# Attention scores from separate products of queries and keys, in place of one product with a matrix fused at setup

## The chip, the core and the metric

The kernel runs on one core of a Trainium2 chip. The metric is device time in microseconds (us) of one launch, inputs and outputs in HBM; lower is better. TensorE is called PE in the rows, its weight loads PEld, VectorE DVE, ScalarE ACT, GpSimd POOL, SyncE (which issues the DMAs) SP.

## The reference, cut to what matters

```python
# x: (2, 2048, 640), ctx: (2, 128, 384); 8 heads of 80; fp32
enc, ca = ctx[:, :124], ctx[:, 124:]                 # 124 text tokens, 4 image tokens
hs = mha(x @ Wq, enc @ Wk, enc @ Wv)                 # text attention
ca_q1 = einsum('btc,th->bch', ca, Wq_ca)[:, indices] # indices: 384 rows spread over 2048
ca_hs1 = mha(ca_q1, x, x)                            # image attention, keys and values are x
ca_hs2 = mha(ca_hs1 @ Wq, ca @ Wk_ca, ca @ Wv_ca)    # 4 keys
out = (hs + ca_hs2) @ Wout + b_out + x
```

`mha` splits the columns by head, scales by 80 ** -0.5, and takes a softmax over the keys.

## The kernel before, in words

One batch entry (an "image", b = 0, 1) is 16 tiles of 128 rows of x. Each image passes through three stages, and setup stands ahead of the first.

**Precision.** Large products run in fp32r. A factor is split into a high part, rounded to fp32r, and a low part, the rest; three products (high x high, low x high, high x low) make one. So each matrix exists as a pair `_hi`, `_lo`: ScalarE writes the high part out of PSUM, VectorE the low one. Setup's products are plain fp32, where one product is two instructions on TensorE.

**Setup** (L1001 to L1057 on TensorE, L559 to L576 on ScalarE, L719 to L763 on VectorE). Scores x @ Wq @ K^T of a head are x @ (Wq_h K_h^T), so setup transposes the context (L1010), makes keys for each head (`kT_part`), transposes Wq (L1039), and multiplies it with the keys of both images: 40 products of 256 columns (L1057). The evictions write `mm_hi` and `mm_lo`, the fused matrix: for each of KT = 5 chunks of 128 rows of x's width it has 2 heads and the columns for g in one part (280 columns), and three heads, with some columns for y, in each of two others (372, 396 or 420 columns). `g_columns` and `y_columns` on GpSimd fill the columns for g (what the image attention needs of Wq_ca) and y (what the last attention needs of its four keys). The part for image 1 is kept in HBM (`raw_kept`) and split in image 0's output stage (`next_high`, `next_low`). The value products of both images (L1147, L1154) are the last of setup.

**Score stage** (`step`, L1103, once per tile). Three parts k = 0, 1, 2, each 5 chunks x 3 products into one PSUM bank; four banks are used in turn. Between those products stand, by a table written by hand (`AT`, L1101): the five transposes of the next tile of x (`xT`, L1070), the two transposes of the stacked g (`g_stack`, L1079), and six "units" (`unit`, L1096), each two products of 256 columns, whose largest value per row VectorE takes (L810). They bound the image attention's scores. After each part VectorE takes the least score per head (`least`, L777), ScalarE copies y (L593) and takes the exponentials with their sums (`exps`, L603), VectorE makes y's low part (L797), and GpSimd multiplies with the reciprocal sums (`normalise`, L492). The result is kept in HBM (`ex_kept`).

**Attention stage** (`sT`, L1194, and `pv`, L1216 and L1225), 32 quads: scores of four heads with 384 rows, exponentials on ScalarE into `e` (L648) and for each second quad into `e_hi` (L654), on VectorE `e_hi` for the others (L893) and always `e_lo` (L901), then products with `ybuf`. First come the transposes of `as_` (L1168), which need all units, and the rows of `aTs` made from them.

**Output stage**: transposed probabilities (`pT`, L1258), products with the value strips `vs_hi`, `vs_lo` (`heads_T`, L1309), with Wout (`output`, L1323), and the sum with x and bias (`add_x`, L958).

Each engine runs its list in the order of the code and waits on semaphores; nothing reorders it. The value strips are made by GpSimd (`value_strips`, L479) inside image b's score stage, after tile 0.

## Time and profile before

| | us |
|---|---|
| median of 3 runs | 797.14 (796.69 to 797.75) |
| the profiled execution, its own time | 797.15 |
| its span, first to last instruction | 795.4 |
| TensorE busy in the span | 772.5 (97%) |
| VectorE busy | 512.6 (64%) |
| ScalarE busy | 371.4 (47%) |
| GpSimd busy | 170.5 (21%) |
| mean granted TensorE clock, share of full speed | 0.991 |

Busy time of TensorE is the sum of modelled durations that overlap, since products are pipelined. What a product costs in a dense stretch is the distance from its start to the next start. In the tables by stage, "PEclk" is the mean of the clock that was granted, as a share of 2.4 GHz (its two levels are 1.2 and 2.4 GHz). The arrow at the end of a row says for how long the engine had been idle, and what ended that.

### The profile page before, as it was taken

How to read it: one execution, taken by the hardware profiler on the slowest of the kernel's cores; microseconds unless marked ns; L12 is line 12 of the kernel's file. 1: busy time of each engine (PE TensorE's matmuls, PEld its weight loads, DVE VectorE, ACT ScalarE, POOL GpSimd, SP SyncE). 2: the span in 40 equal slices, each digit the busy share in tenths (PEclk: the TensorE clock that was granted, in tenths of full speed). 3: DMA queues.
4: the chain of work that ended last, by engine and by line, in shares of the span. 5: the costliest groups of instructions: out<-in, count | busy, mean ns of one | idle time of the engine just before them, and what ended most of it. 6: DMA issues, size and time to landing. Idle time of an engine off the chain costs nothing.

```text
span 795.4 us, 13204 instructions
## 1 busy us (share of the span) xinstructions
PE 772.5 (97%) x5129; PEld 724.1 (91%) x5129; DVE 512.6 (64%) x878; ACT 371.4 (47%) x938; POOL 170.5 (21%) x232
## 2 busy tenths in 40 slices
PE   7999999999899999999999999999989999999998
PEld 5979999999777879999999999999968788999997
DVE  2446777676899986344545777676789996544432
ACT  1634444444489862233233444444469884222220
POOL 7025821222100001332220411222110001212130
PEclk9999999999899999999999999999989999999999
DMA  9123222222220024744422222222230003344431
GB/s 335 70 98 125 87 87 87 87 88 87 86 81 1 1 66 132 240 147 146 165 87 84 87 87 87 88 87 87 100 110 1 1 1 97 119 158 166 148 115 69
DMA packets 33462, 79.34 MB, mean 100 GB/s; under 512 B 8300, under 2 KB 9836, under 8 KB 33400
## 3 DMA queue, kind: packets, MB, share of 16 engines
q1 hardware_dynamic: 33400, 78.49, 29.0%
q8 instruction: 41, 0.67, 0.3%
q14 instruction: 21, 0.17, 0.1%
HBM read 48.56 MB, written 29.88 MB: 99 GB/s over the span
## 4 chain that ended last, share of the span: by engine, by line
PE 92%; DVE 4%; issue 2%; ACT 1%; DMA 0%; SPq 0%; DVEq 0%
PE PS L1124 30%; PE PS L1323 17%; PE PS L1309 8%; PE PS L1096 6%; PE PS L1194 5%; PE PS L1225 5%; PE PS L1216 5%; PE PS L1258 4%; PE PS L1057 2%; PE PS L1070 2%; PE PS L1017 2%; PE PS L1291 1%; DVE e_hi L893 1%; PE PS L1242 1%; PE PS L1079 1%
## 5 line engine op out<-in xcount | busy, mean ns | idle before, releaser
L1124 PE MATMUL PS<-mm_hi,xT_hi 128*128 128x280 f32 (+3 forms) x480 | 161.8, 337 | 0.0
L810 DVE TENSOR_REDUCE mpart<-PS 128x4 f32<-128x512 f32 x192 | 132.0, 688 | 42.0 <-PE PS L1096 41.8
L1124 PE MATMUL PS<-mm_lo,xT_hi 128*128 128x280 f32 (+3 forms) x480 | 157.8, 329 | 0.0
L1124 PE MATMUL PS<-mm_hi,xT_lo 128*128 128x280 f32 (+3 forms) x480 | 157.0, 327 | 0.0
L492 POOL TENSOR_TENSOR ex<-ex,rinv 128x992 f32<-128x992 f32 x32 | 59.1, 1847 | 240.2 <-DVE rinv L804 240.1
L1124 PEld LDWEIGHTS PS<-mm_hi,xT_hi 128*128 128x128 f32 x480 | 90.5, 189 | 0.6 <-issue 0.5
L1124 PEld LDWEIGHTS PS<-mm_hi,xT_lo 128*128 128x128 f32 x480 | 90.6, 189 | 0.3
L1124 PEld LDWEIGHTS PS<-mm_lo,xT_hi 128*128 128x128 f32 x480 | 90.3, 188 | 0.1
L603 ACT ACTIVATE ex<-PS,neg 128x124 f32<-128x124 f32 x256 | 89.9, 365 | 0.1
L901 DVE TENSOR_TENSOR e_lo<-e,e_hi 128x1536 fp32r<-128x1536 f32 (+1 forms) x46 | 77.3, 1689 | 4.9 <-ACT e_hi L654 4.1
L777 DVE TENSOR_REDUCE neg<-PS 128x3 f32<-128x372 f32 (+1 forms) x96 | 47.8, 498 | 48.3 <-PE PS L1124 48.3
L1096 PE MATMUL PS<-gT,aTm 128*128 128x256 f32 x384 | 76.6, 281 | 0.1
L1323 PE MATMUL PS<-wo_hi,oT_hi 128*128 128x320 f32 x320 | 75.4, 317 | 0.0
L1323 PE MATMUL PS<-wo_lo,oT_hi 128*128 128x320 f32 x320 | 72.9, 309 | 0.0
L1323 PE MATMUL PS<-wo_hi,oT_lo 128*128 128x320 f32 x320 | 72.8, 309 | 0.0
L648 ACT ACTIVATE e<-PS 128x1536 f32<-128x1536 f32 x44 | 64.2, 1459 | 14.8 <-PE PS L1194 14.8
L539 POOL TENSOR_TENSOR ex<-p2x,one 128x32 f32<-128x32 f32 x28 | 6.7, 241 | 300.5 <-ACT p2x L677 178.2
L688 ACT ACTIVATE oT_hi<-PS 128x256 fp32r<-128x256 f32 x80 | 30.8, 385 | 84.7 <-PE PS L1309 81.1
L958 DVE TENSOR_TENSOR res<-PS,xin 128x640 f32<-128x640 f32 x32 | 26.3, 823 | 67.9 <-PE PS L1323 67.8
L1194 PE MATMUL PS<-aTs,gT 128*128 128x384 f32 (+2 forms) x384 | 66.8, 314 | 1.9 <-DVE ybuf L797 1.5
L1096 PEld LDWEIGHTS PS<-gT,aTm 128*128 128x128 f32 x384 | 67.6, 188 | 1.2 <-DVE mpart L810 0.5
L593 ACT ACTIVATE ybuf<-PS 128x96 fp32r<-128x96 f32 x64 | 16.2, 254 | 108.9 <-DVE neg L777 108.9
(149 smaller groups left out, 1448.5 us busy)
## 6 DMA issues: line engine op xcount, KB each, us to landing
xin<-in_x SPq DMA_DIRECT2D x64, 320.0 KB, 3.5
ex_kept<-ex SPq DMA_DIRECT2D x32, 512.0 KB, 2.9
ex<-ex_kept SPq DMA_DIRECT2D x32, 512.0 KB, 3.9
out<-res SPq DMA_DIRECT2D x32, 320.0 KB, 2.3
raw_kept<-raw SPq DMA_DIRECT2D x5, 512.0 KB, 2.6
mm_lo<-raw_kept SPq DMA_DIRECT2D x10, 186.0 KB, 3.9
wq_in<-in_L_xattn_Wq SPq DMA_DIRECT2D x2, 800.0 KB, 8.9
wo_in<-in_L_xattn_Wout SPq DMA_DIRECT2D x1, 1600.0 KB, 8.0
```

The source lines that it names most:

```text
L492: nc.gpsimd.tensor_tensor(ex[:, i % 2, :, 0:NK], ex[:, i % 2, :, 0:NK], rinv[:, i % 2, :].unsqueeze(2).broadcast_to([P, NH, NK]), ALU.mult ...
L603: last = nc.scalar.activation(ex[:, i % 2, h, 0:NK], s_ps(T, h), ACT.Exp, bias=neg[:, i % 2, h:h + 1], scale=-1.0, accum_out=sums[:, i % 2 ...
L648: nc.scalar.activation(e_of(p), flat(sT_bank(p), 3), ACT.Exp, scale=SCALE).then_inc(e_made, 1)
L777: nc.vector.tensor_reduce(neg[:, i % 2, h0:h1], PS[:, slot(T, k), at:at + (h1 - h0) * NK].rearrange("p (h k) -> p h k", h=h1 - h0), AX.X, ...
L810: nc.vector.tensor_reduce(mpart[:, n // 2, :, 2 * (n % 2):2 * (n % 2) + 2, i].rearrange("p s k -> p k s"), PS[:, 6 + N % 2, :].rearrange(" ...
L901: nc.vector.tensor_tensor(e_lo[:, p % LO_BUFS, c0:c1], e_of(p)[:, c0:c1], e_hi[:, p % HI_BUFS, c0:c1].bitcast(F32), ALU.subtract)\
L1096: last = mul(PS[:, 6 + N % 2, k * G2:(k + 1) * G2].rearrange("p (s n) -> p s n", s=SETS), aTm[:, r0 + k, c * P:(c + 1) * P], gT[:, :, i * ...
L1124: last = mul(PS[:, slot(T, k), p0:p0 + w], l[:, i % 2, j, :], rr[:, m0:m0 + w], start=(j == 0 and n == 0), stop=(n == 2), skip_group_check ...
L1194: last = mul(flat(sT_bank(p), 3)[:, at:to], gT[:, s, kt * P:(kt + 1) * P], aTs[:, s, r, at - r * CAD:to - r * CAD], start=True, stop=True, ...
L1216: mul(PS[0:y_cols(r), 6 + r // 2, 0:CAD], y_of(kt, s * R + r), e_hi[:, p % HI_BUFS, r * CAD:(r + 1) * CAD], start=(kt == 0 and r % 2 == 0) ...
L1309: last = mul(PS[:, 6 + j % 2, 0:G2], strip(vv, j, h), pp[:, h, :], start=(n == 0 and k == 0), stop=(n == 2 and k + 1 == len(pieces[j])))
L1323: last = mul(PS[:, out_bank(2 * g + u) + f, 0:HALF], l[:, j, u * P:(u + 1) * P], rr[:, j, f * HALF:(f + 1) * HALF], start=(j == 0 and n == ...
```

## The change

Scores are made in two steps, for two tiles at a time (a "group" G, 8 per image). TensorE's order for a group is now:

- `y_part`: y and g of both tiles by themselves, from `yg_hi`, `yg_lo`, which hold for each chunk only the 2 or 3 heads that have rows in it ("pieces", 12 in all), 28 columns each.
- `q_part`: the queries of both tiles, transposed: Wq's chunks are the weights and the two tiles of transposed x the 256 columns. Evicted and split in two as `qT_hi`, `qT_lo`.
- `s_part`: four parts (tile u, heads 0 to 3 or 4 to 7): the transposed queries of a chunk are the weights, and the keys of that chunk's pieces the columns. In a piece the rows of other heads are zero (`headscale` holds the scale in a head's rows and zero in the others).

A unit is one product of 512 columns over both tiles; there are 12 per group, so 96 per image as before in columns, and half the instructions. The fused matrix, its round trip through HBM and the 40 products of setup are gone. Wq itself is split at setup and, since its low part's place is used again by the attention stage, once more for image 1. The value product of image b stands between its score stage and its attention stage, and with it GpSimd's value strips. Tile 1 of image 1 is transposed inside image 0's last output product.

TensorE, cut to the core:

```diff
-                        for j in range(KT):
-                            m0, w = mm_at(j, k)
-                            p0 = ps_at(j, k)
-                            for n, (l, rr) in enumerate(((xT_hi, mm_hi), (xT_lo, mm_hi), (xT_hi, mm_lo))):
-                                last = mul(PS[:, slot(T, k), p0:p0 + w], l[:, i % 2, j, :], rr[:, m0:m0 + w],
-                                           start=(j == 0 and n == 0), stop=(n == 2), skip_group_check=True)
...
+                def y_part(G):
+                    N = b * GROUPS + G
+                    pe.wait_ge(xTl_made, 2 * N + 2)
...
+                    for u in range(2):
+                        for j in range(KT):
+                            at, w = (u * NH + heads[j][0]) * YG, len(heads[j]) * YG
+                            for n, (l, rr) in enumerate(((xT_hi, yg_hi), (xT_lo, yg_hi), (xT_hi, yg_lo))):
+                                last = mul(PS[:, y_bank(N), at:at + w], l[:, u, j, :],
...
+                STACK_AT = 16
+                Q_AT = (32, 38, 44, 50, 56, 62, 68, 74)
+                S_AT = (6, 14, 22, 30)
...
+                def q_part(G):
...
+                    for c in range(KT):
+                        if N * KT + c >= 2:
+                            pe.wait_ge(ql_made, N * KT + c - 1)
+                        for j in range(KT):
+                            for n, (l, rr) in enumerate(((wq_hi, xT_hi), (wq_lo, xT_hi), (wq_hi, xT_lo))):
+                                last = mul(PS[:, q_bank(c), 0:G2].rearrange("p (u n) -> p u n", u=2), l[:, j, c * P:(c + 1) * P], rr[:, :, j, :],
+                                           start=(j == 0 and n == 0), stop=(j == KT - 1 and n == 2))
+                                if at == STACK_AT:
+                                    g_stack(G)
+                                if at in units_at:
+                                    unit(G, units_at.index(at))
...
+                def s_part(G):
...
+                        for c in range(KT):
+                            hs = [h for h in heads[c] if h // R == k]
+                            if not hs:
+                                continue
+                            pe.wait_ge(ql_made, N * KT + c + 1)
+                            m0 = piece_at[c] + heads[c].index(hs[0])
+                            to = hs[0] % R * NK
+                            for l, rr in ((qT_hi, kp_hi), (qT_lo, kp_hi), (qT_hi, kp_lo)):
+                                last = mul(PS[:, s_bank(2 * N + u, k), to:to + len(hs) * NK], l[:, c, u * P:(u + 1) * P],
+                                           rr[:, m0:m0 + len(hs), :].rearrange("p n k -> p (n k)"), start=first, stop=(hs[-1] % R == R - 1 and rr is kp_lo),
...
+                        if G + 1 < GROUPS and p % 2 == 0:
+                            xT(2 * G + 2 + p // 2)
...
+                pe.wait_ge(wv_in_s, (b + 1) * 16)
+                pe.wait_ge(mx_made, (b + 1) * UNITS_B)
+                for c in range(CT):
+                    for f in range(2):
+                        last = mul(PS[0:NK, 6 + f, 0:HALF], ctxT[:, c, b, 0:NK], wv_in[:, c, f * HALF:(f + 1) * HALF],
```

VectorE, the end of a score stage and the new split; GpSimd, where the strips stand:

```diff
+                def q(G, c):
+                    N = b * GROUPS + G
+                    dve.wait_ge(qh_made, N * KT + c + 1)
+                    nc.vector.tensor_tensor(qT_lo[:, c, :], PS[:, q_bank(c), 0:G2], qT_hi[:, c, :].bitcast(F32), ALU.subtract).then_inc(ql_made, 1)
...
+                key_rows(0, 0, 3)
+                inv(TILES - 2)
+                least(TILES - 1, 1)
+                dve.wait_ge(v_ps, b + 1)
+                key_rows(0, 3, R)
+                nc.vector.tensor_copy(v_tok[0:NK, b].rearrange("p (f n) -> p f n", f=2), PS[0:NK, 6:8, 0:HALF]).then_inc(v_made, 1)
+                key_rows(1, 0, R)
                 inv(TILES - 1)
...
-                pool.wait_ge(sc_ps, 3 * (b + 1) * TILES)
+                pool.wait_ge(sc_ps, 2 * (b + 1) * TILES)
+                for half in (vs_hi, vs_lo):
+                    nc.gpsimd.memset(half[:, :].bitcast(F32), 0.0).then_inc(vs_zero, 1)
+                pool.wait_ge(vs_zero, 2 * (b + 1))
+                pool.wait_ge(v_made, b + 1)
                 value_strips(b)
...
+                normalise(b, TILES - 1)
                 nc.gpsimd.memset(vcab[:, :], 0.0).then_inc(vcab_zero, 1)
```

`sT(1)` now waits for all the rows of `aTs` (`aTd_made`, three per image).

**TensorE, inside a tile's score stage, before** (L1124 the fused product, L1096 a unit, L1070 the transposes of the next tile):

```order
L1124 MATMUL PS<-mm_lo,xT_hi 128x420
L1124 MATMUL PS<-mm_hi,xT_hi 128x280
L1124 MATMUL PS<-mm_hi,xT_lo 128x280
L1124 MATMUL PS<-mm_lo,xT_hi 128x280
L1124 MATMUL PS<-mm_hi,xT_hi 128x280
L1096 MATMUL PS<-gT,aTm 128x256 x2
```

All products have 280 to 420 columns; only the seven transposes of a tile have 128.

**TensorE now, from the last score part of a group to the y products of the next** (L1109 transposes the second tile of the next group, L1208 the last scores, L1134 a unit, L1152 y and g):

```order
L1109 MATMUL PS<-ident,xin 128x128 [waits xTl_made,x_in0]
L1109 MATMUL PS<-ident,xin 128x128 x4
L1208 MATMUL PS<-kp_hi,qT_hi 128x124 [waits ql_made,gT_made]
L1208 MATMUL PS<-kp_hi,qT_lo 128x124
L1208 MATMUL PS<-kp_lo,qT_hi 128x124
L1208 MATMUL PS<-kp_hi,qT_hi 128x372 [waits ql_made]
L1134 MATMUL PS<-gT,aTm 128x512 [waits mx_made]
L1208 MATMUL PS<-kp_hi,qT_lo 128x372
L1208 MATMUL PS<-kp_lo,qT_hi 128x372
L1208 MATMUL PS<-kp_hi,qT_hi 128x248 [waits ql_made]
L1208 MATMUL PS<-kp_hi,qT_lo 128x248
L1208 MATMUL PS<-kp_lo,qT_hi 128x248
```

The y products that follow (56 and 84 columns, 30 of them) wait for the split of the tile that was transposed nine products and a unit earlier; before, a tile was transposed some 30 products ahead of its use.

**GpSimd, around the end of image 0's score stage, now** (L460 `normalise`, L490 memsets of the strips, L450 and L454 the strips, L495 the memset of vcab):

```order
L460 TENSOR_TENSOR ex<-ex,rinv 128x8x124 [waits rinv_made] x11
L490 MEMSET vs_hi 128x1280 [waits sc_ps]
L490 MEMSET vs_lo 128x1280
L450 TENSOR_TENSOR vs_hi<-v_tok,one 128x80 [waits v_made,vs_zero]
L450 TENSOR_TENSOR vs_hi<-v_tok,one 128x80 x7
L454 TENSOR_TENSOR vs_lo<-v_tok,vs_hi 128x80 [waits vsh_made] x8
L460 TENSOR_TENSOR ex<-ex,rinv 128x8x124 [waits rinv_made]
L495 MEMSET vcab 32x640
```

Before, the strips stood between tile 0's and tile 1's `normalise`, and only the last `normalise` and the memset of vcab at this place.

## Rows read from the trace of the kernel before

**Rows 1.** The page, busy time by engine (us, share of the span, instructions).

```profile
PE 772.5 (97%) x5129; PEld 724.1 (91%) x5129; DVE 512.6 (64%) x878; ACT 371.4 (47%) x938; POOL 170.5 (21%) x232
```

**Rows 2.** By stage: length, busy PE, PEld, DVE, ACT, POOL, PEclk, DMA, GB/s.

```profile
55.76:210.30 154.54, 153.64 (x1018) 151.50 (x1018) 107.83 (x237) 67.70 (x312) 50.23 (x43) 1.00 0.28 96
210.30:232.00 21.70, 17.95 (x95) 14.65 (x94) 19.44 (x21) 16.15 (x19) 2.41 (x2) 0.84 0.22 81
232.00:296.00 64.00, 61.70 (x386) 51.82 (x385) 59.97 (x46) 55.33 (x43) 0.00 (x0) 1.00 0.05 11
```

**Rows 3.** Timeline of TensorE in one tile: start, us, instruction, columns, count.

```profile
110.06 0.38 PE L1079 MATMUL PS<-ident,gs 128*128 128x128 f32 x2
...
110.79 0.33 PE L1124 MATMUL PS<-mm_hi,xT_hi 128*128 128x372 f32 x1
110.96 0.34 PE L1124 MATMUL PS<-mm_hi,xT_lo 128*128 128x372 f32 x1
...
116.68 0.71 PE L1070 MATMUL PS<-ident,xin 128*128 128x128 f32 x5
...
119.68 0.38 PE L1079 MATMUL PS<-ident,gs 128*128 128x128 f32 x2
```

**Rows 4.** Timeline of TensorE in the attention and output stages.

```profile
261.95 0.97 PE L1194 MATMUL PS<-aTs,gT 128*128 128x384 f32 x6
262.76 0.86 PE L1216 MATMUL PS<-e_hi,ybuf 128*98 128x384 f32 x4
...
318.67 0.52 PE L1309 MATMUL PS<-pT_hi,vs_lo 128*128 128x256 f32 x3
319.02 0.52 PE L1309 MATMUL PS<-pT_lo,vs_hi 128*128 128x256 f32 x3
...
321.01 2.99 PE L1242 MATMUL PS<-p,sel 128*128 128x32 f32 x26
```

**Rows 5.** Timelines of ScalarE and VectorE: the two halves of a tile's split.

```profile
117.42 0.71 ACT L584 ACTIVATE xT_hi<-PS 128x640 fp32r<-128x640 f32 x1 [0.69 <-PE PS L1070]
118.20 0.81 DVE L769 TENSOR_TENSOR xT_lo<-PS,xT_hi 128x640 fp32r<-128x640 f32 x1
```

**Rows 6.** Groups of VectorE instructions: count, busy us, mean ns, idle before.

```profile
L810 DVE TENSOR_REDUCE mpart<-PS 128x4 f32<-128x512 f32 x192 | 132.0, 688 | 42.0 <-PE PS L1096 41.8
L948 DVE TENSOR_TENSOR oT_lo<-PS,oT_hi 128x256 fp32r<-128x256 f32 x80 | 34.0, 425 | 41.6 <-ACT oT_hi L688 41.5
```

**Rows 7.** Timeline of TensorE in setup, to the first score product.

```profile
7.13 7.53 PE L1017 MATMUL PS<-ctxT,wk_in 128*80 128x248 f32 x24 [1.05 <-DVE ctxT L746]
...
14.83 5.18 PE L1017 MATMUL PS<-ctxT,wk_in 128*80 128x248 f32 x24
...
45.88 6.62 PE L1147 MATMUL PS<-wv_in,ctxT 128*124 128x320 f32 x24
...
55.76 0.40 PE L1124 MATMUL PS<-mm_hi,xT_hi 128*128 128x280 f32 x1
```

**Rows 8.** Timelines of TensorE, VectorE and GpSimd: end of the score stage; the strips.

```profile
210.43 0.35 PE L1124 MATMUL PS<-mm_lo,xT_hi 128*128 128x420 f32 x1
...
221.75 0.94 PE L1225 MATMUL PS<-e_lo,ybuf 128*98 128x384 f32 x4 [0.79 <-DVE e_lo L901]
...
217.30 2.60 DVE L893 CAST e_hi<-e 128x1536 fp32r<-128x1536 f32 x1 [0.70 <-ACT e L648]
...
223.28 0.96 DVE L893 CAST e_hi<-e2nd 128x1536 fp32r<-128x1536 f32 x1
...
216.68 1.85 POOL L492 TENSOR_TENSOR ex<-ex,rinv 128x992 f32<-128x992 f32 x1 [9.38 <-DVE rinv L804]
218.46 0.62 POOL L533 MEMSET vcab<- 32x640 f32 x1
...
74.22 2.27 POOL L482 TENSOR_TENSOR vs_hi<-v_tok,one 128x80 fp32r<-128x80 f32 x8
76.45 2.56 POOL L486 TENSOR_TENSOR vs_lo<-v_tok,vs_hi 128x80 fp32r<-128x80 f32 x8
```

More of the change, by code:

```diff
@@ L35 @@
 YC = 2 * YW + 1
-CW = 2 * NK + NH * NT
-STRIDE = 1096
-MMW = KT * STRIDE
+YG = YW + NT
+PW = R * NK
 QUADS = SETS * TILES
@@ new lines, in image_keys, with image_values @@
+            def image_keys():
+                dve.wait_ge(raw_ps, 1)
+                for b, ca in ((0, ca0), (1, ca1)):
+                    nc.vector.tensor_copy(ca[:, :, :], PS[:, 0, 0:KT * NH * B * NT].rearrange("p (q b t) -> p q b t", b=B, t=NT)[:, :, b, :])\
+                        .then_inc(ca_made, 1)
+            def image_values():
+                dve.wait_ge(vca_ps, 1)
+                nc.vector.tensor_copy(v_ca[:, :].rearrange("p (f n) -> p f n", f=2), PS[0:B * NT, 6:8, 0:HALF]).then_inc(vca_made, 1)
@@ L858, in _ @@
-                unit(TILES - 1, HERE)
-                unit(TILES - 1, HERE + 1)
-                least(TILES - 1, 2)
-                unit(TILES - 1, HERE + 2)
+                    image_values()
+                    text_keys()
+                for G in range(GROUPS):
+                    last = G + 1 == GROUPS
+                    g(G)
+                    y_low(2 * G)
+                    y_low(2 * G + 1)
+                    if G:
+                        inv(2 * G - 2)
+                    q(G, 0)
+                    if G == 0:
+                        if b == 0:
+                            dve.wait_ge(z_made, 1)
+                        else:
+                            for u in range(2):
+                                dve.wait_ge(stored[u], b * GROUPS * 16)
+                        nc.vector.memset(ybuf[:, :, :, :].rearrange("p i (m t) d -> p i m t d", t=3)[:, :, :, 1:3, YW].bitcast(F32), 1.0).then_inc(ones_made, 1)
+                    q(G, 1)
+                    units(G, 0, 1, 2)
+                    if G:
+                        inv(2 * G - 1)
+                    q(G, 2)
+                    units(G, 3, 4)
+                    q(G, 3)
+                    units(G, 5, 6, 7)
+                    if not last:
+                        q(G, 4)
+                        units(G, 8)
+                        least(2 * G, 0)
+                        xT(2 * G + 2)
+                        units(G, 9)
+                        least(2 * G, 1)
+                        units(G, 10)
+                        least(2 * G + 1, 0)
+                        xT(2 * G + 3)
+                        units(G, 11)
+                        least(2 * G + 1, 1)
@@ new lines, in _ @@
+            wq_chunk(0)
+            wq_chunk(1)
+            pe.wait_ge(wkca_in_s, 16)
+            pe.wait_ge(aTm_made, R)
+            pe.wait_ge(caT_made, 1)
+            for c in range(KT):
+                for k in range(CT):
+                    last = mul(PS[:, 0, c * B * NT:(c + 1) * B * NT], wk_in[:, 1, k, c * P:(c + 1) * P], caT[:, k].rearrange("p b t -> p (b t)"),
+                               start=(k == 0), stop=(k == CT - 1), skip_group_check=True)
+            last.then_inc(kca_ps, 1)
@@ new lines, in _, with image_keys @@
+            for c in range(2, KT):
+                wq_chunk(c)
+            def image_keys():
+                pe.wait_ge(wqTa_made, 3)
+                pe.wait_ge(wqTd_made, 2)
+                pe.wait_ge(kcap_made, KT)
+                for j in range(KT):
+                    for c in range(KT):
+                        h0, n = heads[c][0], len(heads[c])
+                        at = (j * NH + h0) * B * NT
+                        last = mul(PS[:, 0, at:at + n * B * NT], wqT[:, c, j * P:(j + 1) * P],
+                                   kcap[:, piece_at[c]:piece_at[c] + n, :].rearrange("p n t -> p (n t)"),
+                                   start=(c == 0), stop=(c == KT - 1), skip_group_check=True)
+                last.then_inc(raw_ps, 1)
@@ L1172, in sT @@
+                pe.wait_ge(mx_made, (b + 1) * UNITS_B)
+                for c in range(CT):
+                    for f in range(2):
+                        last = mul(PS[0:NK, 6 + f, 0:HALF], ctxT[:, c, b, 0:NK], wv_in[:, c, f * HALF:(f + 1) * HALF],
+                                   start=(c == 0), stop=(c == CT - 1))
+                last.then_inc(v_ps, 1)
                 def sT(p):
```

836 lines of the change are left out of this document (395 added, 441 removed).

## The prediction

> **What bounds the kernel now.** I read four views in this order. First the page's busy row: TensorE is busy 97% of the span [rows 1]. Busy matmul time overlaps itself, so the second view is the table by stage [rows 2]. In the score stage of image 0 (55.8 to 210.3 us) TensorE has work for 153.6 of 154.5 us, VectorE for 107.8 and ScalarE for 67.7. In the 21.7 us at the stage's end TensorE has gaps, and its mean clock is 0.84; in the attention stage behind it VectorE is busy 60 of 64 us. Third, the TensorE timeline of one tile [rows 3]: the same pair of transposes starts at 110.06 and at 119.68, so a tile takes 9.62 us, and there is no gap in it. In this stage each microsecond of issue time is one of the kernel, 32 times over. Fourth, what one instruction occupies. That is the distance between two starts, not the busy time: a 372-column product takes 110.96 - 110.79 = 0.17 us [rows 3], 0.155 for its columns at 2.4 GHz and 0.015 on top.
>
> **The price of a narrow product** decides this change. Five 128-column transposes, the last with a tail of 0.27 us, fill 0.71 us [rows 3]: 0.11 each. 26 instructions of 32 columns fill 2.99 us [rows 4]: (2.99 - 0.27)/25 = 0.109, hardly less. Both bring 128 new weight columns each time, and that load sets the pace. They are plain fp32. For fp32r there is one witness: six products of 384, 128, 256, 256, 128 and 384 columns take 262.76 - 261.95 = 0.81 us [rows 4]. Two of 384 at 0.175 (their columns and 0.015) and two of 256 at 0.118 (three start in 0.35 [rows 4]) leave 0.22 for two of 128, 0.11 again. So I take 0.11 for each product under some 230 columns. The Trainium skill (TensorE: Matmul & The Clock Gate, Back-to-back issue gap) gives 81 ns for 128 columns; with it the 42 narrow products of a pair of tiles would cost 1.2 us less, and the kernel 20 us less than below. The rows disagree with it.
>
> **The score stage, per pair of tiles.** Before: 2 x 9.62 = 19.24 us. After, in TensorE's order:
> - y and g (L1152): 30 products of 56 or 84 columns, 30 x 0.11 = 3.30.
> - queries (L1174): 75 of 256 columns, 75 x 0.119 = 8.93.
> - scores (L1208): in each of four parts three products of 124, three of 248 and three of 372 columns, 12 x (0.110 + 0.118 + 0.171) = 4.79.
> - units (L1134): 12 of 512 columns. The trace has none; between 0.213 (the columns alone) and 0.236 (two of 256). I take columns and 0.015, 0.228: 2.73.
> - 14 transposes, 14 x 0.11 = 1.54.
>
> Sum 21.29. The columns of y, queries and scores fall from 32448 to 30144, but the products rise from 90 to 141, and 42 of them go at the load's pace: **+2.05 per pair**. To this comes a wait. y_part needs both of its tiles split in two, and the second one is transposed just ahead of the last score part. From the start of its last transpose: 0.27 to land, 0.71 on ScalarE and 0.81 on VectorE [rows 5], three handovers of 0.04: 1.91 us. The cover is 0.11 + 1.20 (nine products) + 0.23 (a unit) = 1.54. I take 0.4 of stall; bounds 0 (quicker handovers) and 1.0 (VectorE still in a 0.69 us reduce [rows 6]). The other new waits I cost at nothing. The transposes of gs stand behind 17 query products, 2.0 us, and VectorE needs some 1.8 us after the last y product for gs and y low. A query chunk's split (0.43 on VectorE [rows 6], about as much on ScalarE) is needed two chunks later, 3.6 us. By engine: VectorE's 107.8 us are 13.4 per pair, and five splits make 15.6 of 21.7; ScalarE goes from 8.5 to some 10.5. If that cover goes, the scores of the chunk are late, and y_part after them.
>
> An image is 7 x 21.69 + (21.29 - 1.10, nothing to transpose ahead) = 172.0 us. Before: 154.9 for image 0 (55.76 to 210.62: the last product starts at 210.43 [rows 7, 8]) and 16 x 9.62 = 153.9 for image 1. **+17.1 and +18.1.**
>
> **Setup.** Before, scores start at 55.76 [rows 7]. The change drops the 80 instructions that multiply keys with the transposed Wq, and takes the value products (24 instructions) out of setup. After, the key products are 30 instructions: 24 take 7.53 us from 7.13, six more at (5.18 - 0.43)/23 = 0.206 [rows 7] end at 15.9. Then three transposes and two chunks of Wq's (13 x 0.11) to 17.3, and 30 narrow instructions for the image keys to 20.6. The last three chunks of Wq pass through evictions of 0.7 to 0.8 us on ScalarE and VectorE, which stand behind the split of Wq itself (two halves of 1600 columns on each, by size 1.5 to 1.8 us): done near 23.4. xT(0) takes 0.55; image_keys, 50 narrow instructions, 5.4, to 29.4; two copies on VectorE 0.8 and POOL's three small operations 1.4, both by size, and POOL's ten masked products at about 0.25 (of the strips eight take 2.27 [rows 8]) to 34.1. xT(1) and the 12 instructions for the image values (0.267 each, as 24 take 6.62 [rows 7]) fit beside that. **-21.7**, bounds -17 and -24, for this chain is laid out by hand. The splits of the text keys hide behind the 12 us of y and queries in the first pair. The memset of ybuf, which a DMA of v_ca releases, ends near 40, when the next query split is not yet due.
>
> **From scores to attention.** The chain: last score, transposes of as_, first exponentials, first e_hi, first e_lo, first product with e_lo. Before, from 210.62 to 221.75 [rows 8]: 11.1 us. After, counted from the last score: transposes 0.7, this image's value products 3.2 and 0.2 to land, one set of key rows 0.5, v_tok 0.8 (now 5.4), the other key rows 1.76: at 7.1 VectorE could start e_hi. But v_tok released POOL at 5.4, with the value strips, 2.27 + 2.56 us [rows 8], then normalise 1.8, then the vcab memset 0.6: busy until 12.6. The row that matters: before, the first e_hi took 2.60 where 0.96 is usual, and it lay across normalise and memset [rows 8]. Its last 0.96 began at 218.94, after normalise's end (218.53): it didn't even get in between the two. The Trainium skill (SBUF — State Buffer, Who interferes with whom) has the rule: a VectorE copy that uses both ports and a GpSimd operation exclude each other for a whole instruction. By this rule, the trace agrees. I take what the row shows: e_hi waits for the last of POOL's chain, 12.6 + 0.96 + 1.76 = 15.3. **+4.2 per image, +8.4.** Bounds: e_hi slips in at once, 9.8, -1.3 per image; or 1 us more per image, since TensorE's clock fell in such a gap before [rows 2].
>
> **Between the images.** The transposes of tile 1 move into the output stage, 0.55. Their split on VectorE stands behind add_x(15), which waits for the last output: 0.35 from the start of its last product, 0.82 for the sum and 0.82 for the split (both 640 columns, as in [rows 5]), less 0.14 that passes anyway: 1.85 of gap where there was none. **+2.4**, bounds 0.5 and 3. Splitting Wq and rescaling the text keys for image 1 takes 17 small operations on each of two engines where 15 stood, in a stage where both are half idle: nothing. The attention and output stages are otherwise the same code.
>
> **Sum**, against the profiled execution's own 797.15 us (span 795.4; 0.01 over the median of the runs, 797.14): 797.15 - 21.7 + 17.1 + 18.1 + 8.4 + 2.4 = **821.5**.
>
> **Rivals.**
> 1. POOL hardly holds VectorE up. For: a strip has 80 columns, and e_hi may get its turn between two of sixteen. Against: e_hi waited across an instruction boundary. 821.5 - 2 x 5.5 = 810.5. Chance 0.25.
> 2. The stall grows: query splits, reduces and exponentials meet in the last score parts, and VectorE coming one reduce (0.6) later is passed on to y_part 14 times. For: VectorE has nine operations there with hardly a break. Against: it is idle a quarter of the pair. 830 or more. Chance 0.15.
> 3. The other side: narrow fp32r products are priced by columns and not by the load, 0.015 + columns/2400. Then y costs 1.3 instead of 3.3 and the 12 products of 124 columns 0.5 less, 2.5 per pair, 40 in all: 781. It decides from 1.5 us less per pair. Against: 0.11 in three kinds of row. Chance 0.06.
> 4. The change doesn't give back what it says at setup: a load or POOL's chain holds the first scores until 45. 832. Chance 0.05.
>
> **How the numbers follow.** The forecast has 0.45 (the rest, 0.04, is what I haven't thought of); with errors of 4 at setup, 4 in the stalls and 3 at the borders it spans 814 to 829. Rivals 1, 2 and 4 extend that to 806 and 835, which leaves out under 2 in 10. About 0.2%, 1.6 us, is what a measurement of this kernel can tell from no change. Faster: rival 3, 0.06; same 0.03; slower 0.91.
>
> **What would show it.** Scores from 34 on; y products 0.11 apart; pairs 21.7 apart, with a gap of 0.4 ahead of y that VectorE's split of a tile ends; a first e_hi of some 5 us beside POOL's strips; 2 us of gap before image 1. The forecast is wrong if y products are 0.04 to 0.08 apart, if pairs are 23 or more apart, or if e_hi keeps to 0.96 beside POOL.

## The result, and the profile after

The changed kernel takes 849.25 us (median of 4 runs, 847.41 to 851.32) against 797.18 for the kernel before: the ratio is 1.065, with a 95% interval of 1.063 to 1.068. The forecast was 821.5, with a range of 806 to 835. So the direction was right, and the time lies above the range. The profiled execution took 851.3 us, the longest of the four, with a span of 849.3 where the kernel before has 795.4. One of the four executions of e5_halves, below, ran at a mean clock of 0.55 and took 1281 us; it isn't in that kernel's ratio, and without it the median is 828.5 and not 828.8.

The page of the changed kernel, busy time and the granted clock in 40 slices of 21.2 us:

```profile
PE 819.6 (96%) x5672; PEld 766.2 (90%) x5672; DVE 534.1 (63%) x876; ACT 381.4 (45%) x940; POOL 191.5 (23%) x236
...
PEclk9599999999999999999997999899999999999999
```

TensorE is busy for 96% of the span, where it was for 97% [rows 1]: it works for 47 us more, and the row doesn't say on what. The clock row has a 5 in its second slice, which is setup, and a 7 at the start of image 1. The table by stage, with the columns of [rows 2], cut here at the start of each pair's y_part in image 0, shows more:

```profile
16.00:20.40 4.40, 4.40 (x42) 4.33 (x41) 2.56 (x2) 2.03 (x2) 0.68 (x5) 1.00 1.04 396
20.40:25.30 4.90, 4.01 (x22) 3.39 (x22) 1.25 (x6) 1.41 (x2) 0.00 (x0) 0.57 0.94 359
25.30:35.90 10.60, 10.60 (x53) 10.60 (x51) 0.82 (x1) 0.70 (x1) 0.00 (x0) 0.50 0.01 3
35.90:42.65 6.75, 6.75 (x19) 2.27 (x19) 1.38 (x3) 4.45 (x16) 3.75 (x14) 0.58 0.00 0
42.65:64.50 21.85, 21.67 (x168) 20.87 (x167) 17.68 (x42) 6.74 (x24) 2.77 (x1) 1.00 0.18 52
64.50:86.40 21.90, 21.62 (x168) 20.91 (x168) 15.05 (x32) 10.04 (x45) 9.75 (x7) 1.00 0.23 82
86.40:109.70 23.30, 23.11 (x167) 22.38 (x167) 14.91 (x32) 9.96 (x44) 11.29 (x7) 0.93 0.20 72
109.70:133.10 23.40, 23.13 (x168) 22.40 (x168) 15.03 (x32) 10.07 (x45) 3.69 (x2) 0.93 0.21 75
...
443.50:470.10 26.60, 26.34 (x168) 25.62 (x168) 13.87 (x29) 6.80 (x25) 0.00 (x0) 0.81 0.18 55
```

There are two kinds of pair. Some take 21.9 us at full clock; others, with the same instructions, take 23.3 at a mean clock of 0.93 (in image 1 the first takes 26.6 and one more 24.9). The forecast knew only the first kind. The low stretch lies behind y_part, as the table over one pair (PE alone, then PEclk, DMA, GB/s) and the timeline there show:

```profile
86.40:89.50 3.10, 3.10 (x28) 0.98 0.14 54
89.50:92.90 3.40, 3.40 (x17) 0.51 0.00 0
92.90:96.30 3.40, 3.40 (x30) 1.00 0.38 154
```

```profile
42.65 0.29 PE L1152 MATMUL PS<-yg_hi,xT_hi 128*128 128x56 f32 x1
...
46.02 0.37 PE L1174 MATMUL PS<-xT_hi,wq_hi 128*128 128x256 f32 x1
...
89.07 0.29 PE L1152 MATMUL PS<-yg_hi,xT_hi 128*128 128x84 f32 x1
89.19 0.29 PE L1152 MATMUL PS<-yg_hi,xT_lo 128*128 128x84 f32 x1
...
89.42 0.39 PE L1152 MATMUL PS<-yg_hi,xT_hi 128*128 128x56 f32 x1
89.64 0.39 PE L1152 MATMUL PS<-yg_hi,xT_lo 128*128 128x56 f32 x1
...
91.06 0.41 PE L1174 MATMUL PS<-xT_hi,wq_lo 128*128 128x256 f32 x1
91.28 0.41 PE L1174 MATMUL PS<-xT_lo,wq_hi 128*128 128x256 f32 x1
```

The first two rows are the first pair's y_part, 30 products in 3.37 us, 0.112 each. In the third pair TensorE is never idle either. It issues narrow products for 3 us. Then the granted clock goes from 2.4 to 1.2 GHz, the last narrow products are 0.21 apart, and the query products behind them 0.22 where 0.12 is usual. Some 3.4 us later the clock is back. One such stretch costs 1.5 us (23.3 less 21.8).

**The difference by stage**, from starts in the two timelines (us; the forecast beside it, where the row has a term there):

| | before | after | difference | forecast |
|---|---|---|---|---|
| to the first product of the score stage | 55.76 | 42.65 | -13.1 | -21.7 |
| score stage, image 0, to the start of its last product | 154.7 | 181.6 | +27.0 | +17.1 |
| from there to the first output product | 94.5 | 96.9 | +2.4 | +4.2 |
| output, image 0, to image 1's first y product | 120.0 | 122.4 | +2.4 | +2.4 |
| score stage, image 1 | 153.5 | 184.8 | +31.3 | +18.1 |
| to the first output product | 94.5 | 96.9 | +2.4 | +4.2 |
| output, image 1, to the start of its last product | 118.7 | 120.2 | +1.5 | 0 |

At 1.2 GHz the kernel spends 20.5 us in setup, 17.1 in image 0's score stage (five stretches), 23.9 in image 1's (10.2, 3.4, 6.8 and 3.4), and 3.4 in the last output stage. Behind each score stage come 3.4 us more, where the kernel before has 6.8: those were its only ones. So a low stretch lies behind nine of the 16 blocks of y_part.

### The profile page after: what moved, and what is told of

Same layout as the page of the kernel before. It is cut to its first block, busy times and chain, and to the rows that moved or that the text cites. A ratio compares the mean times of both kernels' runs of the same rounds, so it can differ in the third digit from the quotient of the medians.

```text
span 849.3 us, 14298 instructions
## 1 busy us (share of the span) xinstructions
PE 819.6 (96%) x5672; PEld 766.2 (90%) x5672; DVE 534.1 (63%) x876; ACT 381.4 (45%) x940; POOL 191.5 (23%) x236
## 4 chain that ended last, share of the span: by engine, by line
PE 86%; DVE 7%; ACT 3%; issue 3%; DMA 1%; SPq 0%; DVEq 0%
PE PS L1174 18%; PE PS L1391 16%; PE PS L1375 7%; PE PS L1152 7%; PE PS L1208 7%; PE PS L1134 5%; PE PS L1291 4%; PE PS L1261 4%; PE PS L1282 4%; PE PS L1324 3%; PE PS L1109 2%; DVE e_lo L921 2%; DVE xT_lo L778 1%; PE PS L1085 1%; ACT xT_hi L560 1%
## 5 line engine op out<-in xcount | busy, mean ns | idle before, releaser
L824 DVE TENSOR_REDUCE mpart<-PS 128x2 f32<-128x512 f32 x192 | 131.4, 687 | 15.5 <-PE PS L1134 12.5
L460 POOL TENSOR_TENSOR ex<-ex,rinv 128x992 f32<-128x992 f32 x32 | 61.3, 1915 | 313.5 <-DVE rinv L813 313.5
L1174 PE MATMUL PS<-xT_hi,wq_hi 128*128 128x256 f32 x400 | 120.5, 301 | 0.0
L1174 PE MATMUL PS<-xT_lo,wq_hi 128*128 128x256 f32 x400 | 119.7, 299 | 0.0
L1174 PE MATMUL PS<-xT_hi,wq_lo 128*128 128x256 f32 x400 | 119.1, 298 | 0.0
L1174 PEld LDWEIGHTS PS<-xT_hi,wq_lo 128*128 128x128 f32 x400 | 82.2, 206 | 4.6
L1174 PEld LDWEIGHTS PS<-xT_hi,wq_hi 128*128 128x128 f32 x400 | 82.2, 206 | 0.3
L1174 PEld LDWEIGHTS PS<-xT_lo,wq_hi 128*128 128x128 f32 x400 | 81.8, 204 | 0.3
L1134 PE MATMUL PS<-gT,aTm 128*128 128x512 f32 x192 | 77.1, 401 | 1.2 <-DVE mpart L824 1.2
L674 ACT ACTIVATE oT_hi<-PS 128x256 fp32r<-128x256 f32 x80 | 30.7, 383 | 82.6 <-PE PS L1375 79.0
L818 DVE TENSOR_TENSOR qT_lo<-PS,qT_hi 128x256 fp32r<-128x256 f32 x80 | 33.1, 414 | 53.9 <-ACT qT_hi L572 52.5
L1261 PEld LDWEIGHTS PS<-aTs,gT 128*128 128x128 f32 x384 | 58.4, 194 | 8.6 <-issue 4.5
```

What stands on the lines that cost most here:

```text
L460: nc.gpsimd.tensor_tensor(ex[:, i % 2, :, 0:NK], ex[:, i % 2, :, 0:NK], rinv[:, i % 2, :].unsqueeze(2).broadcast_to([P, NH, NK]), ALU.mult ...
L824: nc.vector.tensor_reduce(mpart[:, n // R, :, n % R, G], PS[:, 6 + N % 2, :].rearrange("p (s n) -> p s n", s=SETS), AX.X, ALU.max)\
L1134: mul(PS[:, 6 + N % 2, :].rearrange("p (s n) -> p s n", s=SETS), aTm[:, r, c * P:(c + 1) * P], gT[:, :, G * G2:(G + 1) * G2], start=True, ...
L1174: last = mul(PS[:, q_bank(c), 0:G2].rearrange("p (u n) -> p u n", u=2), l[:, j, c * P:(c + 1) * P], rr[:, :, j, :], start=(j == 0 and n == ...
L1261: last = mul(flat(sT_bank(p), 3)[:, at:to], gT[:, s, kt * P:(kt + 1) * P], aTs[:, s, r, at - r * CAD:to - r * CAD], start=True, stop=True, ...
```

## The experiments

Theory N: long stretches of narrow products, though TensorE never pauses in them, lower its clock, and that is most of what the forecast missed. Before, no product of the score stage but the seven transposes of a tile had under 256 columns. The rival at the start was G: the 0.2 us gap ahead of y_part, which is also new, does it. All diffs are against the changed kernel. "Half" in the table is the time at 1.2 GHz within a stage, "score" runs from the first product of the score stage to the start of its last score product.

| | median | ratio to before (95%) | first product | half, setup | score 0 (half) | score 1 (half) |
|---|---|---|---|---|---|---|
| the change | 849.25 | 1.065 (1.063 to 1.068) | 42.65 | 20.5 | 181.6 (17.1) | 184.8 (23.9) |
| e1_y_wide | 835.91 | 1.048 (1.045 to 1.052) | 41.92 | 20.5 | 176.0 (0) | 176.0 (0) |
| e2_early_xT | 840.06 | 1.054 (1.051 to 1.057) | 41.78 | 20.5 | 177.9 (13.7) | 181.1 (20.5) |
| e3_border | 844.28 | 1.059 (1.055 to 1.063) | 39.54 | 10.2 | 181.6 (17.1) | 183.1 (20.5) |
| e5_halves | 828.84 | 1.039 (1.036 to 1.043) | 41.70 | 20.5 | 173.2 (0) | 173.3 (0) |
| e4_values | 859.71 | 1.077 (1.074 to 1.081) | 47.99 | 37.6, to 58 us | 186.4 (17.1) | 184.7 (23.9) |
| e10_y_high | 798.80 | 1.002 (1.000 to 1.003) | 41.03 | 17.1 | 158.3 (0) | 157.6 (3.4) |

(In e4_values the 37.6 us run on into the first pair; its 17.1 counts the five later stretches alone.)

**1. Wide products in y_part's place (e1_y_wide).**

```diff
-    at, w = (u * NH + heads[j][0]) * YG, len(heads[j]) * YG
+    at, w = u * (2 * NH * YG - G2), G2
...
-               rr[:, piece_at[j]:piece_at[j] + len(heads[j]), :].rearrange("p n d -> p (n d)"),
+               rr[:, :, :].rearrange("p n d -> p (n d)")[:, 0:w],
```

> The change, with y_part's 30 products widened from 56 or 84 columns to 256 (they read the first 256 columns of yg_hi or yg_lo, so y and g are no longer those of the reference; all else, the number of products and every wait, is as in the change). Theory N (what drops TensorE's clock to 1.2 GHz behind y_part is the stretch of narrow products, 3.3 us at 0.11 each): the nine drops in the two score stages go, 18.4 us back (7.6 and 10.8), less 30 x (0.119 - 0.11) = 0.3 per pair, 16 times, 4.3: about 835, with pairs of 22.1 to 22.2 and the granted clock 1.00 behind y_part. Theory G (the 0.2 us gap ahead of y_part drops it): the gap is still there, so the drops stay: 849 + 4 = 853 us. Setup's drop stays by both.

Measured: 835.9, and both score stages entirely at full clock, in the table of TensorE over each of them (the columns as above):

```profile
41.92:217.92 176.00, 173.81 (x1326) 1.00 0.21 73
438.83:614.83 176.00, 173.81 (x1326) 1.00 0.21 75
```

More columns, and less time. Pairs are 22.08 apart, all 14 of them, and the gap ahead of y_part is still there (0.23, and 1.65 ahead of image 1). This leaves N and ends G, as a cause by itself.

**2. The gap away (e2_early_xT).** The second tile's transposes come after the third score part's third product, at 20 in the count of products, and VectorE splits it ahead of unit 10 and the least score.

```diff
+                                if at == XT_AT and G + 1 < GROUPS:
+                                    xT(2 * G + 3)
...
-                        if G + 1 < GROUPS and p % 2 == 0:
-                            xT(2 * G + 2 + p // 2)
+                        if G + 1 < GROUPS and p == 0:
+                            xT(2 * G + 2)
```

> The change, with the transposes of a pair's second tile (and its split on VectorE) seven products earlier in the third score part, so that y_part of the next pair finds it split. Both theories: the 0.22 us gap ahead of y_part goes, 14 x 0.22 = 3 us. Theory N (narrow stretch): the drops behind y_part stay, though perhaps not in the same pairs: 844 to 848 us. Theory G (gap): those behind the pairs go too (image 1's first, behind the 1.65 us gap, stays): 849 - 3 - 13.7 = 832.

Measured: 840.1, four below N's range and eight above G's 832. The gap is gone in all 14 pairs. Pairs at full clock went from 21.83 to 21.53, and there are still low stretches, behind four pairs in image 0 and four in image 1, where the change had five and four with one longer. So the gap isn't needed for a low stretch. Low stretches were 6.8 us shorter in all, which accounts for 3 us beside the 4 of the gaps. The output stage of image 1 had none this time (118.7 instead of 120.2), 1.5, and setup was 0.9 shorter.

**3. The same work in another order (e5_halves).** This is the decisive run, since nothing is left out or added. Beside y_part the places of the stacked g and of the units move back, and ScalarE and VectorE take the first query chunk ahead of y and g.

```diff
-                def y_part(G):
+                def y_part(G, u):
...
-                    pe.wait_ge(xTl_made, 2 * N + 2)
+                    pe.wait_ge(xTl_made, 2 * N + 1 + u)
...
+                    pe.wait_ge(xTl_made, 2 * N + 2)
                     for c in range(KT):
+                        if c == 1:
+                            y_part(G, 1)
...
-                    y_part(G)
+                    y_part(G, 0)
                     q_part(G)
```

> The change, same products, in another order: y_part is cut in two, 15 products of the first tile, then the 15 query products of chunk 0 (256 columns), then the 15 of the second tile; stack transposes and units move back with it. No stretch of more than 15 narrow products is left in the score stage. The gap ahead of y_part goes as well, since its first half needs only the first tile. Theory N: no drops in the score stages, 18.4 back, and 3 for the gaps: 828 us, pairs of 21.7; up to 3 us more if VectorE, which has eight reduces in the last 36 query products, holds the units up. Theory G: also no drops; this run tells whether they can be had back with all the work done. Theory A (all that a drop needs is that the narrow products are there, in any order, as the mean over the pair): the drops stay, 846.

Measured: 828.8. Over the two score stages, first the changed kernel, then this one (all engines, PEclk after POOL):

```profile
42.65:224.30 181.65, 179.45 (x1327) 173.57 (x1326) 122.05 (x261) 75.17 (x314) 42.27 (x25) 0.95 0.20 71
443.53:628.31 184.78, 182.59 (x1325) 176.77 (x1326) 118.16 (x248) 75.08 (x314) 27.20 (x15) 0.94 0.20 71
```

```profile
41.70:214.90 173.20, 172.97 (x1327) 166.23 (x1327) 122.94 (x261) 75.44 (x315) 42.26 (x25) 1.00 0.21 74
433.90:607.20 173.30, 172.97 (x1327) 166.14 (x1327) 120.61 (x250) 75.53 (x315) 27.22 (x15) 1.00 0.22 76
```

The same number of instructions, 8.4 and 11.5 us less, clock 1.00. Pairs are 21.67 apart. N holds: with 15 narrow products, then 15 of 256 columns, then 15 narrow ones TensorE kept its clock in all 16 pairs; with 30 narrow ones in a row it lost it in nine of 16 (the change) and in eight (e2_early_xT). Theory A falls with it.

**4. The border between the images (e3_border).**

```diff
                             next_xT()
+                            dve.wait_ge(xTh_made, (b + 1) * TILES + 2)
+                            dve.wait_ge(xbias, (b + 1) * TILES)
+                            nc.vector.tensor_tensor(xT_lo[:, 1].rearrange("p k n -> p (k n)"), flat(4)[:, 0:H],
+                                                    xT_hi[:, 1].bitcast(F32).rearrange("p k n -> p (k n)"), ALU.subtract).then_inc(xTl_made, 1)
                     add_x(2 * g_ + 1)
```

> The change, with VectorE's split of image 1's second tile ahead of the sum of the last tile of image 0 instead of behind it (and behind the last bias sum of GpSimd, whose row shares memory with it). The gap of 1.65 us ahead of image 1's first y_part goes. If only the gap was lost, -1.7: 847.6. If the 10.2 us at 1.2 GHz that follow (444.4 to 454.6) are due to gap and narrow products together (theory GN), 4.7 us more come back, or 3.2 if a drop of the usual 3.4 us stays: 843 to 844.5.

(`xT(1)`, VectorE's split of tile 1, now stands in image 0's score stage alone.) Measured: 844.3, inside the range, but only in part for the reason given. Behind gap and narrow products together the clock had been low for 10.2 us, without the gap it was for 3.4, and image 1's first pair went from 26.55 to 23.36, as GN said. The gap is gone:

```profile
443.53 0.29 PE L1152 MATMUL PS<-yg_hi,xT_hi 128*128 128x56 f32 x1 [1.65 <-DVE xT_lo L778]
```

```profile
439.91 0.46 PE L1395 MATMUL PS<-wo_hi,oT_lo 128*128 128x320 f32 x2
440.25 0.29 PE L1156 MATMUL PS<-yg_hi,xT_hi 128*128 128x56 f32 x1
```

(The first row is the changed kernel's, the other two this one's.) But its 1.7 us don't show in the length of the output stage, 122.2 against 122.4, since this execution had a low stretch of 3.4 us there, at 337.5, worth 1.5. In the same way image 1 gained one in a later pair, and its output stage lost the one that the changed kernel has. And 3.1 us came from setup, where the low stretch lasted 10.2 us instead of 20.5, though no instruction of setup was changed: that gives a reading of setup. First the changed kernel, then this one, TensorE alone:

```profile
25.35 10.69 PE L1085 MATMUL PS<-kcap,wqT 128*128 128x16 f32 x50
...
37.12 5.60 PE L1094 MATMUL PS<-wvca_in,caT 128*8 128x320 f32 x12
```

```profile
25.16 9.06 PE L1089 MATMUL PS<-kcap,wqT 128*128 128x16 f32 x50
...
35.30 4.31 PE L1098 MATMUL PS<-wvca_in,caT 128*8 128x320 f32 x12
```

With 10.2 us fewer at 1.2 GHz the first y product came 3.1 us earlier. With none TensorE would be ready for it at 34.4 (39.54 less half of 10.2, an estimate), but GpSimd's chain ends later: in e4_values, where nothing covers it, the first y product comes 4.7 us behind the last of the image keys (43.3 to 47.99), and at full clock these would end near 30.7. So it would come at about 35.4, an estimate too; the forecast had 34.1. How long the clock stays low in setup differs between kernels whose setup is the same: 20.5 us in the change, 17.1 in e9_pieces, 10.2 here and in e6_strips. No run shows why.

**5. Wide products among the narrow ones of setup (e4_values).** `image_values()` is dissolved: its products stand in `image_keys`.

```diff
                                    start=(c == 0), stop=(c == KT - 1), skip_group_check=True)
+                        n = j * KT + c
+                        if n % 4 == 0 and n // 4 < 2 * CT:
+                            image_value(n // 4)
                 last.then_inc(raw_ps, 1)
```

> The change, with the six image value products of setup (320 columns, plain fp32, 12 instructions) no longer behind the image keys' 25 groups of two instructions but between them, one after each fourth product. Theory N (narrow stretches drop the clock and wide ones keep it): image keys and values run at 2.4 GHz for at least part of their 8.6 us; what is exposed then is GpSimd's chain behind the keys (0.6 + 3.9 us): first y product at 38 to 40 instead of 42.65, 845 to 847. Theory N2 (one wide product in five is too few to lift a clock that has fallen before, at 21 us): all 50 instructions at 1.2 GHz, keys done at 42.5, first y product at 46 to 47, 853.

Measured: 859.7, N2's side and worse. The table over setup, TensorE alone:

```profile
20.50:25.00 4.50, 3.52 (x19) 0.55 1.04 394
25.00:43.10 18.10, 18.10 (x63) 0.50 0.00 1
43.10:48.00 4.90, 1.39 (x8) 0.50 0.00 0
48.00:58.00 10.00, 10.00 (x47) 0.50 0.21 70
```

The clock had already fallen (21 us), and the mixture, one wide product in every five, didn't lift it. In the changed kernel it came back at 41.6, 4.5 us into the closed block of value products; here only in the first pair's query products. And GpSimd's chain now lies open ahead of y_part, 3.5 us of idle time. What brings the clock down in setup was not tested by itself.

**6. What the narrow products themselves cost (e10_y_high).**

```diff
-    for n, (l, rr) in enumerate(((xT_hi, yg_hi), (xT_lo, yg_hi), (xT_hi, yg_lo))):
+    for n, (l, rr) in enumerate(((xT_hi, yg_hi),)):
```

> The change, with y_part's low-high and high-low products left out (10 products per pair instead of 30; y and g lose their low parts, all else stays). The price of a narrow product and the clock's drop stand against each other: 20 x 0.112 = 2.24 us per pair, 35.8 in all, and, by theory N (a long narrow stretch drops the clock), the nine drops with 18.4: 849.3 - 54.2 = 795, pairs of 19.6, granted clock 1.00 throughout the score stages. If the narrow products only cost their load and the drops had another cause: 813.5. If they are priced by columns (0.04 each) and all the rest is the drop: 831 minus 12.8, 818.

Measured: 798.8, 50.5 us less, where 54.2 was expected; the ten executions of this kernel go from 796.1 to 801.6. The spans of the profiled ones differ by 53.7 (849.3 to 795.6), but that this is near 54.2 is luck: 50.5 of it lie in the score stages, and 3.1 come from shorter low stretches in setup and the last output stage. Pairs are 19.58 apart, 21.83 less 20 x 0.112. What is missing in the score stages is the very first pair, which kept its 21.88, since TensorE now waits 2.1 us there for VectorE, ahead of the transposes of the stacked g, and one low stretch. The 20 products that are gone cost 0.112 each, and not the 0.04 to 0.05 of rival 3: this is rival 3's end. The clock was low once in the score stages, for 3.4 us in image 1's first pair, behind the border's gap. Without two thirds of y_part the changed kernel is as fast as the kernel before.

**7. GpSimd in the attention stage (e9_pieces, e6_strips).** The first cuts the last tile's `normalise` into eight instructions; the second cuts the strips to 2 columns of 80.

```diff
-                normalise(b, TILES - 1)
+                normalise_heads(b, TILES - 1)
```

```diff
-    nc.gpsimd.tensor_tensor(vs_hi[:, strip_at[h]:strip_at[h] + D], v_tok[:, b, h * D:(h + 1) * D], ones([P, D], 0), ALU.mult)\
+    nc.gpsimd.tensor_tensor(vs_hi[:, strip_at[h]:strip_at[h] + 2], v_tok[:, b, h * D:h * D + 2], ones([P, 2], 0), ALU.mult)\
```

> The change, with GpSimd's normalise of each image's last tile in eight instructions (one head, 124 columns each) instead of one of 992 columns; same work. It runs beside VectorE's attention stage. Theory L (VectorE waits for the end of the GpSimd instruction that is under way, so a long one costs it its length: e_hi took 3.17 instead of 0.96 at 246.73, e_lo 3.28 at 647.84): 1.5 to 2 us per image come back, 845.5 to 846. Theory S (the many short strips ahead of it are what slows VectorE in this stage): no change, 849.

> The change, with GpSimd's value strips at the attention stage's start cut to 2 columns of their 80 (so the values are not those of the reference; 16 instructions as before, but near nothing to do). The stage from the last score product to the first output product took 94.46 us in the kernel before and 96.9 in the change. Theory S (the strips, which stretched from 4.8 to 14.6 us beside VectorE, took the 2.4 us): 94.5, 844.5 us in all. Theory L (normalise and the memset behind them, two instructions of 1.85 and 0.62, hold up two VectorE instructions by 2.2 and 1.5): they only come 10 us earlier, where they hit the first e_hi as in the kernel before: 96 to 97, 847 to 849.

Measured: 848.2 and 846.5. How many low stretches an execution has blurs the medians, so the stage itself is read. From the last score product to the first output product it took 96.85 and 96.92 us in the changed kernel; it is 95.98 and 95.42 with the pieces and 95.82 and 95.66 with the short strips. The seven other kernels whose code is the change's in this stage have 96.8 to 97.0 in image 0 and 96.4 to 97.4 in image 1, so a single figure of image 1 is good to half a us; image 0 of the short strips had 3.4 us more at 1.2 GHz here than the change. e11_best, with the pieces too, has 95.4 in both images. Neither theory is right alone: the strips cost some 1.0 to 1.3 us per image, and `normalise` in one piece 0.9 to 1.5. VectorE and GpSimd in the changed kernel:

```profile
231.47 0.91 DVE L913 CAST e_hi<-e 128x1536 fp32r<-128x1536 f32 x1
...
242.04 1.11 DVE L913 CAST e_hi<-e 128x1536 fp32r<-128x1536 f32 x1
...
246.73 3.17 DVE L913 CAST e_hi<-e 128x1536 fp32r<-128x1536 f32 x1
...
230.61 4.57 POOL L450 TENSOR_TENSOR vs_hi<-v_tok,one 128x80 fp32r<-128x80 f32 x8
235.15 10.05 POOL L454 TENSOR_TENSOR vs_lo<-v_tok,vs_hi 128x80 fp32r<-128x80 f32 x8
245.16 3.36 POOL L460 TENSOR_TENSOR ex<-ex,rinv 128x992 f32<-128x992 f32 x1
```

And with the pieces:

```profile
241.84 12.57 POOL L461 TENSOR_TENSOR ex<-ex,rinv 128x124 f32<-128x124 f32 x8
```

Beside short GpSimd instructions VectorE's cast takes 0.91 to 1.15, and it is GpSimd that stretches: the strips from 2.27 and 2.56 [rows 8] to 4.57 and 10.05, and the eight pieces take 12.57, where the whole in one instruction takes 1.85 alone. Beside one long instruction the cast takes 3.17.

**8. Repairs put together (e7_all, e11_best).**

> The change with y_part in two halves (as in the run of that name), VectorE's split of image 1's second tile ahead of the last sum, and in the very first pair the query products of chunk 0 ahead of y_part, while GpSimd's chain and the clock's low stretch of setup pass. All the work is done. From 828.8 of the halves: -1.7 for the gap between the images, -1.8 where the 15 query products fill a wait, or less if they run at 1.2 GHz: 825.5 to 827. If it reaches below 797 (the kernel before), the change would be worth it; by the sum of the pairs (21.67 against 19.24, 16 times) it can't.

e7_all, with all the work done, is e5_halves with the VectorE lines of e3_border and, in the very first pair, `y_part` behind the query products of chunk 0. Measured: 827.2, ratio 1.037 (1.034 to 1.040). The gap was already gone in e5_halves, whose first half needs only the first tile; what came back in the output stage (122.1 to 120.6) is a low stretch that e5_halves had at 330.8 and this run hadn't. The first pair gave nothing: the first query split waits on ScalarE for the copy of v_ca, and another 3.4 us at 1.2 GHz came at 49 us. This pair is the only one in which all 30 narrow products stand in a row again (45.00 to 48.27), and the only one with a low stretch, as N has it. The other pairs stay at 21.67.

> The change with y_part's low parts left out (as in the run with the high products alone, so y and g lose their low parts), and three of the repairs that keep all work: the second tile transposed seven products earlier, VectorE's split of image 1's second tile ahead of the last sum, and GpSimd's last normalise in eight pieces. From that run's 798.8: 14 gaps of 0.22 = 3.1, the gap between the images 1.7, and 0.9 + 1.5 in the attention stages: 791.6, that is 0.8% below the kernel before (797.5). If a repaired gap only lets something else be late (VectorE's reduces in the last score part), 793 to 796.

e11_best is e10_y_high with e2_early_xT, e3_border and e9_pieces; it leaves out y's and g's low products. Measured: 791.9 (nine executions, 787.5 to 795.0), ratio 0.992 (0.990 to 0.995). It is 0.8% below the kernel before, which makes all the products. The score stages are 156.4 and 157.6. Pairs are 19.30 apart; the gap between the images went, but image 1's first pair now waits 1.9 us ahead of the transposes of the stacked g in its place, as the very first does.

## Why the prediction was wrong

- **What failed** is that no term had a clock. "50 narrow instructions, 5.4" and the pair's sum priced everything at 2.4 GHz; the clock appeared only as a bound of 1 us per image at the border, since the kernel before shows a low clock only in that gap [rows 2]. The table above gives the sum: in setup the image keys took 10.7 instead of 5.4 and the values 5.6 instead of 3.2, with the transposes 8 us; in image 0 five stretches of 1.5, 7.5; in image 1 first pair 4.7, two of 1.5 and one of 3.1, 10.8; in the last output stage 1.5. Not all of setup's 8 reach the first score: by the estimate above it would come at 35.4 at full clock, so the clock cost 7.3 there. That makes 27 of the 29.8 us between the forecast's difference (24.4) and that of the profiled executions (54.2). The rest is 1.3 more in setup at full clock, 2.4 more in each score stage, and 3.6 less behind them. What the range lacked was a rival in which the *kind* of work lowers the clock.
- **The sum of a pair** was sound at full clock. It said 21.29 for issue; without gap and low clock e2_early_xT measures 21.53, so 0.24 was missing. Per product: y (46.02 - 42.65)/30 = 0.112 for 0.110, queries 0.120 for 0.119, the unit of 512 columns 108.66 - 108.43 = 0.23 for 0.228. The stall was 0.23 for 0.4. Forecast 21.69, measured 21.83. An image without low stretches is 173.2 (e5_halves) for 172.0.
- **Rival 3** (fp32r priced by columns) is excluded by e10_y_high, and by the y products themselves, 0.112 apart. The 81 ns for 128 columns of the Trainium skill (TensorE: Matmul & The Clock Gate, Back-to-back issue gap) don't show in this case's traces either: it is 0.11 at full clock and 0.21 at half.
- **Setup**: the chain as laid out gives 34.1 at full clock; the estimate from e3_border and e4_values is 35.4, since the image keys start at 25.35 and not at 24.0.
- **From scores to attention** was wrong in the mechanism. The forecast let the first e_hi wait for the whole of GpSimd's chain; it took 0.91 beside the strips, as rival 1 had it and as the prediction's own sign of being wrong says, and the first e_lo product came 10.7 us behind the last score (and 11.2 in image 1), not 15.3:

```profile
224.29 0.28 PE L1208 MATMUL PS<-kp_lo,qT_hi 128*128 128x248 f32 x1
...
235.00 1.39 PE L1291 MATMUL PS<-e_lo,ybuf 128*98 128x384 f32 x4
```

  But the cost did not vanish: it came 15 us later, 2.4 per image, about half of it where e_hi or e_lo meets `normalise`. The Trainium skill (SBUF — State Buffer, Who interferes with whom) says that one waits for a whole instruction of the other; of single instructions the rows agree, and the forecast stretched it to a chain of 18.
- **Between the images**: +2.4, as forecast (a gap of 1.65 for 1.85). What it overlooked is that this gap, with y_part behind it, makes the longest low stretch of the score stages.
- **Rivals 2 and 4** both named a real lateness (pairs of 23.3, and a first product at 42.65, where 4 had 45) with the wrong cause: the stall was no longer than forecast, and no load was late.

## What to carry to other kernels

Price the clock as well as the instructions: when a change collects narrow products (here 30 of 56 or 84 columns, 3.4 us) into a block, ask what TensorE's clock does behind it, though the engine never idles, and look first whether the block can be cut by wide products that stand there anyway. Here that was worth 20 us of 849 with the same work (22 between the profiled executions, 18 of them the clock's and most of the rest for gaps). And a new gap of TensorE next to such a block costs more than its length.

A narrow product costs more than its columns: here 0.11 us with 8, 32, 56, 84 or 128 of them. Each brings 128 new weight columns, and the load of these is the likely price; the changed kernel's four products with 98 weight columns at 310.9, 0.08 apart, point the same way, but no run tests it. Merging 30 such products into others, or leaving them out, is worth more than the columns say (here 2.24 us per pair for 20). What makes a pair slower in every execution (21.67 against 19.24, 39 us over 16 pairs) was countable before, and none of the orders tried here brings it back (the best is 21.53).

## What the runs showed of the hardware

- TensorE's clock fell from 2.4 to 1.2 GHz without idle time ahead, behind a block of narrow products (89.4 us in the change; in e2_early_xT without any gap ahead of the block). It stayed low for 3.4 us where wide products followed at once, in one pair of the change for 6.8, and for 10.2 where a gap of 1.65 us stood ahead of the block. In setup, among 50 narrow plain fp32 instructions, it stayed low for 20.5 us.
- A narrow product's price follows the clock: 0.112 us at full and 0.213 at half, and so does a 256-column one's, 0.12 and 0.213. At half clock 56 columns and 256 columns cost the same.
- Not every block does it. In the changed kernel pairs 1, 2 and 6 of image 0 and four of image 1 stayed at full clock with the same instructions. And the 26 narrow instructions of the output stage, 2.99 us in both kernels [rows 4], had no low stretch behind them in either image of the profiled execution before, and one in image 1 after (the timeline, and TensorE's table around it); e1_y_wide, e3_border and e5_halves had one in image 0 instead.

```profile
741.35 2.99 PE L1308 MATMUL PS<-p,sel 128*128 128x32 f32 x26
```

```profile
739.00:744.50 5.50, 5.50 (x50) 1.00 0.38 140
744.50:748.00 3.50, 3.50 (x16) 0.54 0.02 5
```

What decides between two equal blocks is left open. Executions of one kernel differ in how long the clock is low: in the ten of e10_y_high the mean clock is 0.989 in the shortest (796.1 us) and 0.981 in the longest (801.6).
- GpSimd's short instructions grew up to fourfold beside a busy VectorE (the low strips, 2.56 to 10.05 us), while VectorE lost 0.04 to 0.2 us per instruction. `normalise` took 12.57 in eight pieces there and 1.85 alone in one; what part of that is the cutting itself no run shows.
